# A decoder kernel whose experts' token lists are built by one-hot products, with a gather per tile in place of scatters

## The reference

```python
gate_logits = x @ gate_w + gate_b                       # 8 experts
weights, indices = jax.lax.top_k(gate_logits, 2)
weights = softmax(weights)
h = einsum('bsd,edh->ebsh', x, w1) + b1                 # 128 -> 1024
xh, gh = split(h, 2)
out_e = einsum('ebsf,efd->ebsd', silu(gh) * xh, w2) + b2
sel = take_along_axis(out_e, indices)                   # the two chosen experts
return sum(sel * weights)
```

## Time and profile before

| | us |
|---|---|
| median of 3 runs (826.69 to 833.39) | 828.49 |
| the profiled execution, its own time | 834.13 |
| its span in the trace | 832.0 |

### The profile page before, as it was taken

The page is one execution under the profiler, slowest core; times in us unless marked ns, Lnnn a source line. Parts: engine busy times, 40 slices in busy tenths (PEclk is TensorE's granted clock), DMA queues, the critical chain, the costliest instruction groups (busy, mean ns, idle before and its releaser), DMA issues.

```text
span 832.0 us, 14945 instructions
## 1 busy us (share of the span) xinstructions
PE 676.5 (81%) x4693; PEld 328.5 (39%) x4698; DVE 589.4 (71%) x1606; ACT 414.0 (50%) x708; POOL 282.6 (34%) x502
## 2 busy tenths in 40 slices
PE   2758998989888896079999952677999989998987
PEld 1324454435344444045666631222332323324443
DVE  3857788776556765657878745788889898953574
ACT  1332665655655542013333312156788777885454
POOL 4742454544523144703223220122323142331310
PEclk9875999989988858579999985569999999999898
DMA  7543654482233215211111123321223011000000
GB/s 218 159 175 119 208 181 142 137 274 72 70 99 87 74 42 156 77 33 40 44 41 40 45 68 126 101 77 52 65 90 127 27 52 51 3 2 1 2 25 26
DMA packets 74780, 71.27 MB, mean 86 GB/s; under 512 B 14560, under 2 KB 67168, under 8 KB 74704
## 3 DMA queue, kind: packets, MB, share of 16 engines
q1 hardware_dynamic: 72000, 64.84, 25.3%
q0 software_dynamic: 2272, 4.69, 1.8%
q10 hardware_dynamic: 432, 0.79, 0.3%
HBM read 41.90 MB, written 28.00 MB: 84 GB/s over the span
## 4 chain that ended last, share of the span: by engine, by line
PE 60%; DVE 19%; issue 7%; DMA 5%; POOL 4%; ACT 4%; SPq 1%; DVEq 0%; POOLq 0%; ACTq 0%
PE bank_pv L733 11%; DVE mx L591 11%; PE bank_turn L575 8%; PE bank_scores L2025 5%; PE bank_scores L685 4%; PE bank_scores L1775 4%; PE bank_turn L1760 4%; PE bank_scores L1760 4%; PE bank_turn L752 3%; POOL routed_tokens L1727 2%; PE bank_scores L1768 2%; PE bank_turn L528 2%; DVE stats L450 1%; DMA stk<-stack_A 1%; PE bank_turn L794 1%
## 5 line engine op out<-in xcount | busy, mean ns | idle before, releaser
L591 DVE TENSOR_REDUCE mx<-bank_turn 128x1 f32<-128x512 f32 (+3 forms) x452 | 260.4, 615 | 58.8 <-PE bank_turn L580 29.6
L575 PE MATMUL bank_turn<-stk 64*128 64x128 bf16 (+3 forms) x708 | 164.2, 322 | 31.2 <-DVE mx L591 20.4
L685 PE MATMUL bank_scores<-stk 64*128 64x512 bf16 (+4 forms) x576 | 176.3, 373 | 4.7 <-ACT probs L706 3.6
L710 ACT ACTIVATE probs<-bank_scores 128x1024 f32<-128x1024 f32 (+4 forms) x160 | 116.9, 769 | 101.6 <-PE bank_scores L685 100.3
L706 ACT ACTIVATE probs<-bank_scores 128x512 f32<-128x512 f32 x256 | 138.6, 605 | 35.5 <-PE bank_scores L685 34.5
L733 PE MATMUL bank_pv<-probs,vsl 128*32 128x512 f32 (+4 forms) x1152 | 142.9, 570 | 2.6 <-POOL probs L718 1.6
L575 PEld LDWEIGHTS bank_turn<-stk 64*128 64x128 bf16 x708 | 58.2, 101 | 133.4 <-DVE mx L591 63.9
L718 POOL TENSOR_SCALAR_AFFINE_SELECT probs<-probs 128x256 f32<-128x256 f32 x128 | 51.6, 408 | 72.3 <-ACT probs L710 70.7
L1743 POOL DMA_INDIRECT expert_outputs<-probs,y_at x39 | 37.3, 958 | 101.4 <-DVE probs L1662 98.8
L477 POOL TENSOR_TENSOR rstd<-var,mhalf 128x4 f32<-128x4 f32 x24 | 25.4, 1056 | 115.8 <-DVE var L456 115.7
L1807 ACT COPY okT<-bank_scores 128x512 f32<-128x512 f32 x39 | 22.9, 587 | 81.2 <-PE bank_scores L1768 81.2
(11 more groups left out here) (297 smaller groups left out, 1140.9 us busy)
## 6 DMA issues: line engine op xcount, KB each, us to landing
stk<-stack_A SPq DMA_DIRECT2D x64, 256.0 KB, 3.3
w<-in_M_w SPq DMA_DIRECT2D x12, 512.0 KB, 4.9
stack_A<-parts SPq DMA_DIRECT2D x15, 384.0 KB, 3.1
stack_A<-fill SPq DMA_DIRECT2D x8, 512.0 KB, 5.3
stk<-stack_X SPq DMA_DIRECT2D x16, 256.0 KB, 2.7
stack_A<-parts SPq DMA_DIRECT2D x15, 256.0 KB, 3.3
probs<-routed_tokens SPq DMA_DIRECT2D x39, 65.0 KB, 1.9
b_gated<-in_M_b SPq DMA_DIRECT2D x1, 2048.0 KB, 11.2
```

The costliest lines, as they stand in the source:

```text
L575: mm = e.matmul(o, stk[r, slot, 0, pp, qt * P:(qt + 1) * P], stk[r, slot, 1, pp, 0:keys], start=True, stop=not a.causal)
L591: e.tensor_reduce(o.rearrange("p h q -> p q h"), bank_of((g, m))[:, 0:k * wide].rearrange("p (q h k) -> p q h k", q=len(tiles), h=len(hs)) ...
L685: mm = e.matmul(score_bank(g, kt, i)[0:a.kp, 0:S - q0], stk[r, slot, 1, pp, kt * P:kt * P + a.kp], stk[r, slot, 0, pp, q0:S], start=True, ...
L710: e.activation(probs[0:a.kp, probs_of(g, kt), j:HG:2, 0:n], bank_scores[0:a.kp, 2 * j:2 * j + 2, 0:n], ACT.Exp, scale=1 / math.sqrt(HD)).t ...
```

## The change

The rows are no longer sorted in DRAM. SP writes the normalised rows to DRAM in token order, four plain DMAs (`rows_sp`). What is sorted are their numbers: for each (tile, choice) two one-hot matrices are made, one over the tile number of the place (`of_e`) and one over the place within the tile, scaled by the row's return address (`of_p`), and PE sums the 32 products of them in one bank (`index_pe`), which gives a table of 128 tiles x 128 places. The marks of batches 0 to 2 are made on POOL, those of batch 3 on DVE (`marks_of`). ACT copies the table out, one more product picks the 40 tiles (`select_pe`), and DVE takes from it the return addresses `y_at` and the rows to read, `x_at_row`. Each tile then gathers its 128 rows with an indirect DMA from POOL into one of three buffers, and the scatter of the results follows on the same queue. The gate weights and the ternary weights, which were computed ahead of the loop, are computed one step per tile inside it. The regions' padding and its DMAs are gone.

```diff
-SCATTER_IN = {28: 0, 29: 1, 30: 2, 31: 3}
+ROWS_IN = {25: 0, 29: 1}
+MARK_IN = {28: 0, 29: 1, 30: 2, 31: 3}
...
             gate_pe(e, 2)
+            index_pe(e, 0)
             norm_pe(e, M0.ln, 3)
             rank_pe(e, 2)
+            index_pe(e, 1)
             gate_pe(e, 3)
             rank_pe(e, 3)
+            index_pe(e, 2)
+            index_pe(e, 3)
...
             rank_dve(e, 3)
+            for t in range(QT * (NB - 1), NT):
+                marks_of(e, t)
...
             norm_pool(e, M0.ln, 2)
-            for t in range(QT, QT + 2):
-                scatter_pool(e, t)
+            for t in range(QT, 2 * QT):
+                marks_of(e, t)
             norm_pool(e, M0.ln, 3)
-            for t in range(QT + 2, NT):
-                scatter_pool(e, t)
+            for t in range(2 * QT, 3 * QT):
+                marks_of(e, t)
...
-            e.tensor_copy(place_u[:, :, tiles], place_f[:, :, tiles]).then_inc(m["placed"], 1)
+            e.tensor_scalar(place_r[:, :, tiles], place_f[:, :, tiles], 1.0 / P, ROUND, ALU.mult, ALU.add).then_inc(m["placed"], 1)
...
+            e.tensor_scalar(place_e[:, :, tiles], place_r[:, :, tiles], -ROUND, None, ALU.add).then_inc(m["placed"], 1)
...
+            e.scalar_tensor_tensor(place_p[:, :, tiles], place_e[:, :, tiles], -float(P), place_f[:, :, tiles], ALU.mult, ALU.add)\
...
+        def marks_of(e, t):
...
+            for k in range(2):
+                e.tensor_scalar(of_p[:, q, k], iota_edge[:], place_p[:, k, t:t + 1], row_at[:, t, k:k + 1],
+                                ALU.is_equal, ALU.mult)
+                i = e.tensor_scalar(of_e[:, q, k], iota_n[:], place_e[:, k, t:t + 1], None, ALU.is_equal)
+            i.then_inc(m["marked" if b < NB - 1 else "marked_last"], 1)
+
+        def index_pe(e, b):
...
+            for q in range(QT):
+                e.wait_ge(m["marked"], QT * b + q + 1) if b < NB - 1 else e.wait_ge(m["marked_last"], q + 1)
+                for k in range(2):
+                    i = e.matmul(bank_pv[:, 0:P], of_e[:, q, k], of_p[:, q, k], start=(b + q + k == 0),
+                                 stop=(b == NB - 1 and q == QT - 1 and k == 1), skip_group_check=True)
+            i.then_inc(m["indexed"], 1)
+
+        def select_pe(e):
...
+            e.matmul(bank_pv[:, P:P + MT], table[:], tile_sel[:], start=True, stop=True).then_inc(m["y_rows"], 1)
...
-            weights_dve(e)
+            e.wait_ge(m["y_rows"], 1)
+            e.tensor_tensor(y_at[:], bank_pv[:, P:P + MT], iota_t[:], ALU.max).then_inc(m["y_at"], 1)
+            e.wait_ge(m["y_at"], 1)
+            e.tensor_scalar(x_at_row[:], y_at[:], 1, NT * P - 1, ALU.logical_shift_right, ALU.bitwise_and).then_inc(m["x_at"], 1)
...
                 output(t, ex)
+                if t == 2:
+                    gates()
+                weights_dve(e, t - 3)
...
         def moe_pool(e, ln):
 
+            e.wait_ge(m["rows"], 16 * NB)
+            e.wait_ge(m["x_at"], 1)
+            for t in range(IN_FLIGHT):
+                gather_pool(e, t)
             for t in range(BUSY_TILES):
-                e.wait_ge(m["y_at"], t + 1)
+                if t + IN_FLIGHT < BUSY_TILES:
+                    e.wait_ge(m["xT"], t + 1)
+                    gather_pool(e, t + IN_FLIGHT)
                 e.wait_ge(m["y_out"], FREE + t + 1)
                 e.indirect_dma_start(scr_y, bass.IndirectOffsetOnAxis(ap=y_at[:, t:t + 1], axis=0),
                                      y_sb[:, t % 2], None).then_inc(m["stored"][t % 2], 16)
 
+        def gather_pool(e, t):
+            n = t % IN_FLIGHT
+            e.indirect_dma_start(x_in[:, n], None, scr_xn, bass.IndirectOffsetOnAxis(ap=x_at_row[:, t:t + 1], axis=0))\
+                .then_inc(m["tile_in"][n], 16)
...
         def moe_act(e, ln):
+            e.wait_ge(m["indexed"], NB)
+            e.copy(table[:], bank_pv[:, 0:P]).then_inc(m["table"], 1)
```

More of the change, by code:

```diff
@@ L36 @@
 BUSY_TILES = MT - 1
[L37 to L41, removed]
+REGION = NT * P
+EDGE = (P - 1) / 2
+DUMP = 2 * NT * P
+IN_FLIGHT = 3
 CODED = 4
@@ L1145, in unit_pool @@
                     beside_pool(e, g, step)
[L1146 to L1149, removed]
+            if g in MARK_IN:
+                marks_of(e, MARK_IN[g])
         def unit_sp(e, g):
@@ L1496, in build @@
         m = {n: sem(f"M0_{n}") for n in """logits top top_at top_f picked routed sum_in
-            place placed zero_at zeros tokens floor cum tile_le tile_held tile_f tile_at tile_row tile_e y_at
-            diff expo plus recip gates zeroed scattered xT xT_out gated_half gated plain_half plain silu act actT actT_out y_in y_out
+            place placed marked marked_last indexed table rows floor cum tile_le tile_held tile_f tile_at tile_sel tile_e y_rows y_at x_at
+            diff expo plus recip gates xT xT_out gated_half gated plain_half plain silu act actT actT_out y_in y_out
             weighed""".split()}
-        m |= {n: [sem(f"M0_{n}{i}") for i in range(2)] for n in ("tile_in", "stored")}
+        m |= {n: [sem(f"M0_{n}{i}") for i in range(2)] for n in ("stored",)}
+        m["tile_in"] = [sem(f"M0_tile_in{i}") for i in range(IN_FLIGHT)]
         m["got"] = [sem(f"M0_got{i}") for i in range(NB)]
@@ L1710, in build @@
         y_sb = probs[:, 0, 2:4, 0:D]
-        x_in = probs[:, 1, 0:2, 0:ROW]
+        x_in = probs[:, 1, 0, 0:IN_FLIGHT * D].rearrange("p (n d) -> p n d", n=IN_FLIGHT)
         x_inT = probs[:, 1, 2:4, 0:P]
@@ L1980, in weights_dve @@
                 e.tensor_scalar(w[k], w[k], f_inv[:, k:k + 1], ROUND, ALU.mult, ALU.add).then_inc(f["q1"], 1)
-            e.wait_ge(f["q1"], 2)
-            for k in range(2):
+            elif step in (9, 10):
+                k = step - 9
+                e.wait_ge(f["q1"], 2)
                 e.tensor_scalar(w[k], w[k], -ROUND, 1.0, ALU.add, ALU.min).then_inc(f["q2"], 1)
-            e.wait_ge(f["q2"], 2)
-            e.tensor_scalar(w[0], w[0], -1.0, f_mean[:, 0:1], ALU.max, ALU.mult).then_inc(f["q3"], 1)
@@ L1986, in weights_dve @@
-            e.tensor_scalar(f_w2q[:].rearrange("p c d -> p (c d)"), w[1], -1.0, None, ALU.max).then_inc(f["q3"], 1)
-            e.wait_ge(f["q3"], 2)
-            for k in range(3):
+            elif step == 11:
+                e.wait_ge(f["q2"], 2)
+                e.tensor_scalar(w[0], w[0], -1.0, f_mean[:, 0:1], ALU.max, ALU.mult).then_inc(f["q3"], 1)
+            elif step == 12:
+                e.tensor_scalar(f_w2q[:].rearrange("p c d -> p (c d)"), w[1], -1.0, None, ALU.max).then_inc(f["q3"], 1)
+            elif step in (13, 14, 15):
+                k = step - 13
+                e.wait_ge(f["q3"], 2)
```

147 lines of the change are left out of this document (76 added, 71 removed).

## The result

The changed kernel takes 852.51 us (median of 4 runs, 844.54 to 853.25), the kernel before 829.12 beside it: a ratio of 1.0255, 95% interval 1.018 to 1.0329. By the ratio it is slower by 21 us (15 to 27); the two medians lie 23 apart. The profiled execution took 852.0, with a span of 850.2 (before: 834.13 and 832.0).

A forecast was written before the change was run, and what follows sets the result against it. PE was taken to bound the loop, 124.23 of 126 us busy. The loop's +13.0 and the front's +1.2 make 14.2, which on the 828.5 median gives 842.7 us; range 825 to 855.

The forecast's parts named there:

- likeliest case: Whole kernel: gathers queued behind scatters land late and the front grows slightly, 14.2 us more in sum; chance 0.65.
- loop term: Expert loop: each gather behind a scatter lands 0.74 late, 0.37 more a tile over 35 gathers, +13.0 us.
- rival of slow gathers: Loop: gathers land as slowly as the last scatter, 3.10 us, so 1.54 late, giving 857 us; chance 0.10.
- The front: Stretch before the loop, to the second tile's landing: scatters out, marks, products and tile arithmetic in, +1.2 us (-5.5 to +6.3).
- Marks ahead of the last deviation: Front, POOL: batch 1's 16 marks delay the last deviation and so DVE's normalisation, +1.5 us.
- Products ahead of the gate: Front, PE: eight index products at half clock stand ahead of the last gate, +4.1 us.
- 16 marks on VectorE: Front, DVE: batch 3's marks follow the last ranking at 0.28 us each, +4.5 us.
- Tile arithmetic: Front: arithmetic on the tiles, formerly hidden under scatters, is now on the path, 4.5 us plus 0.5 for two more instructions.
- Interference of VectorE and POOL: Front: DVE's last gate and ranking and POOL's batch 2 marks slow each other, +2.9 us.
- The weights' steps in the loop: Loop, DVE: fifteen weight steps, one per tile, fit between the result and the next gate half, costing nothing.
- gather in time: Loop: gathers land within 1.56 us, the pace stays at 3.23 and only the front counts, 829.7 us; chance 0.15.
- collapse: Front: gather in time, and index products hold PE at full clock with cheap marks, giving 821 us; chance 0.10.

The follow-up runs named there:

- e3: Changed kernel with a row of its own for each empty slot, instead of one row shared by a tile's empty slots: 844.51 us, ratio 1.0182.
- e5: The changed kernel run again without any edit: 852.65 us, ratio 1.0253.
- e4: Changed kernel with PE's one-hot products of batches 1 and 2 moved behind the last gate and its ranking: 848.7 us, ratio 1.022.
- e6: Changed kernel with eight experts' numbers per code word instead of four, so five register reads instead of ten; row numbers made earlier: 848.48 us, ratio 1.0231.
- e1: Changed kernel with only POOL's order altered, the gather of tile t+5 issued before the scatter of tile t: 831.53 us, ratio 1.0038.
- e10: Changed kernel with e1, e3, e4 and e6 joined, the last deviation ahead of two tiles' marks, one more tile's marks on DVE: 825.65 us, ratio 0.9934.

## Why the prediction was right, and where its sizes were off

The mechanism was the one forecast: a gather queued behind a scatter closes a circle over two tiles, and PE stands for rows. The likeliest case gave +14.2 on the profiled execution, 848.3; the profiled execution after took 852.0, 17.9 more, and the two stretches account for 17.7 + 0.9 = 18.6. The median forecast, 842.7, is 9.8 below the measured 852.5, which lies near the upper end of the range, 855. The layers behind the loop differ by some us from profile to profile (338.5 to 343.3 us from the last scatter to the end), so the 23 us between the medians are not accounted for more closely than this.

**The loop term, +13.0, was mis-sized; it measured 17.7.** The steady circle is 7.15 against the 7.20 forecast, but that is luck in part, since two errors cancel: a scatter starts 0.27 after its result, not 0.76 (why it is quicker here was not tried), and the gather with its hand-over takes 2.6, not 2.3; scatter to gather 1.29 (1.26) and turning to result 2.97 (2.88) are near. 35 gathers x (3.57 - 3.23) = 12. What the term left out is that landing times differ from tile to tile: it took one for all 39. Ten of them landed in 3.2 to 4.0. Seven are tiles of mostly empty slots, 3.2 us of loop (e3; 4.4 against e5). The other three, tiles 9, 20 and 31 (3.2, 3.8, 4.0), each had an instruction fetch in the DMA queues at the same time. For tile 31 the queues from 466.7 to 470.7 us show it (packets, MB, share of the engines):

```profile
q0 software_dynamic: 64, 0.13, 11.3%
q8 instruction: 1, 0.02, 2.3%
```

In e3, where the empty slots are cured, tiles 9, 14, 20, 26 and 31 took 3.0 to 3.8, again each beside such a fetch, and its loop is 137.35 - 122.85 - 12 = 2.5 us over the steady circle. But a fetch alone does not do it: the gathers of tiles 15 and 26 of the changed kernel also had one beside them and landed in 2.54 and 2.57. The cause of these late landings stays open. The rival of slow gathers (3.10 each, 857) was right in number for a quarter of the tiles, though not for its reason, a product on DVE: the gather at 449.13 was issued beside one and took 2.57.

**The front, +1.2, measured 0.9, by errors that cancel.** From the variance on:

- Marks ahead of the last deviation: forecast +1.5, measured 5.15 - 2.21 = 2.9. The two-scalar mark cost 0.81 as taken from the earlier trace rows, the one-scalar mark 0.59 to 0.62 where the row of another operation gave 0.377.
- Products ahead of the gate: +4.1 forecast, +2.9 measured (e4 gets 2.9 back at the gate). They ran at half clock as forecast (granted 0.50), but in 3.76 for eight, not 4.6, and the gate had waited about 0.5 at that place anyway.
- 16 marks on VectorE: 4.5 forecast, 341.25 to 345.17 = 3.9. Tile arithmetic 5.0 forecast, 345.17 to 349.75 = 4.6.
- Interference of VectorE and POOL: +2.9 forecast from the earlier trace rows, about 0.4 found. The last gate and ranking took 6.55 us (334.67 to 341.22) against 5.78 before, of which 0.4 are the two new steps. The variance, 0.57 instead of 0.17, adds another 0.4 ahead of the point from which I measure. The reading of the earlier trace rows was too high as well: it puts VectorE's 3.84 down to two POOL instructions, and two more (lines 818 and 658) ran beside it.
- Not in the sum at all: TensorE's ten register reads, some 6.4 us, once hidden under scatters, now on the path, for 1.9 (e6). The sum gave the last landing as the end and did not ask what else PE needs. The second gather was late too, started 1.55 behind the first and landed in 3.17 (1.26 and 2.3 forecast), but the reads ended later still.

**The weights' steps in the loop, taken as free, are free**: with PE at its bound (e1) one pitch of 38 is 3.45, the last 2.76 and the rest 3.22 to 3.32. The three scatters that took 1.18 instead of 0.98 stood beside three of these steps, the tensor_tensors that make `f_w1c`; beside the six quantising steps scatters took 0.98 to 0.99. The Trainium skill, "SBUF — State Buffer", section "Who interferes with whom", by which a DVE instruction that holds the port pair it shares with GpSimd makes GpSimd wait for the whole of it, would have allowed up to 2.0 us for the six, by the prediction's estimate. No run here tests that: in e1 these steps and the scatters' issues overlapped by 0.1 us at most.

The Trainium skill, "DMA: Bandwidth & Descriptors", section "Anatomy of one DMA", by which a write to HBM waits longest for its receipt, would have a gather land ahead of a scatter. This trace has it the other way: gathers 2.5 to 2.6, scatters 2.3.

The rival "gather in time" is refuted by the 22 waits, the "collapse" by the products' half clock and a front that did not shrink. e10 shows that a front 7 us shorter was there to be had, by order and fewer register reads; PE's granted clock was 0.75 and 0.61 there (327 to 333 and 333 to 338 us).

## What to carry to other kernels

On a queue that runs in order, count the tiles of lead not by buffers but by what stands ahead of the load: issue it when its buffer is free, ahead of the store of an older tile. The circle's length divided by the tiles of lead gives the pace, where that is longer than the busiest engine's own work on a tile, and it shows before any run. When work that hid other work is removed, list everything that ran under it, register reads too, and ask which of it the first consumer needs.

## What the runs showed of the hardware that was not expected

- An indirect gather of 128 rows of 512 B whose descriptors name one and the same row 88 to 128 times landed in 3.2 to 3.5 us, with rows of their own in 2.4 to 2.7 (e3). Scatters likewise: 2.8 to 3.1 us to one row, 2.2 to 2.3 to rows of their own. With 41 equal rows the difference was 0.2.
- A read of a register from SBUF took TensorE's queue 0.30 us (median of ten); with the two register instructions behind it a register cost 0.64, ten of them some 6.4 (e6).
- POOL issued an indirect DMA in 0.97 to 0.98 us, 1.29 after the one before, gather or scatter alike; three scatters beside a tensor_tensor of VectorE took 1.18.
- On POOL, comparing 128 x 128 numbers with one scalar per partition took 0.59 to 0.62 us, 1.6 times the 0.377 of an addition and a multiplication with one scalar.
